# Two dense products per tile in the last full chunk, and a short last chunk that works on its five columns and rows alone

## The reference

```
x = layernorm(x + L0(x))     # three GCN convolutions with elu, then a linear map
W   = einsum('rb,bio->rio', w_comp, bases)              # 8 relations from 4 bases
msg = x[src] * edge_weight
agg = segment_sum(msg, edge_type * N + dst)             # per relation and node
x = layernorm(x + einsum('rni,rio->no', agg, W))
```

## Time and profile before

| | |
|---|---|
| time, median of 3 runs | 1186.85 us |
| profiled execution, its own time | 1187.31 us |
| its span (first to last instruction) | 1185.5 us |
| second layer's gathers, first start to last start | 541.0 to 1168.8 us |
| TensorE busy in 541 to 1170 us | 603.20 of 629.00 us |
| last output's norm on VectorE ends | 1182.72 us |

### The profile page before, as it was taken

The page is one execution under the profiler, slowest core; times in us unless marked ns, Lnnn a source line. Parts: engine busy times, 40 slices in busy tenths (PEclk is TensorE's granted clock), DMA queues, the critical chain, the costliest instruction groups (busy, mean ns, idle before and its releaser), DMA issues.

```text
span 1185.5 us, 21211 instructions
## 1 busy us (share of the span) xinstructions
PE 1076.2 (91%) x6601; PEld 833.6 (70%) x6604; DVE 836.3 (71%) x1992; ACT 684.9 (58%) x1716; POOL 543.1 (46%) x579
## 2 busy tenths in 40 slices
PE   2678888899999999977899999999999999999997
PEld 2565555566544644576788898888888888888885
DVE  4789889995566647787666767677676767767654
ACT  1598888984200310049666677677667767666740
POOL 5052000000132000005777777777777777777773
PEclk9778889999999999998999999999999999999999
DMA  6162000000200100214222212222222222222221
GB/s 165 34 233 92 1 2 1 1 1 1 66 23 12 49 7 4 60 35 112 53 53 58 58 52 58 57 56 53 57 56 55 55 57 55 53 58 55 57 54 36
DMA packets 49230, 60.66 MB, mean 51 GB/s; under 512 B 15255, under 2 KB 38841, under 8 KB 48502
## 3 DMA queue, kind: packets, MB, share of 16 engines
q0 software_dynamic: 17456, 36.02, 11.6%
q1 hardware_dynamic: 31686, 23.61, 6.8%
HBM read 46.30 MB, written 8.49 MB: 46 GB/s over the span
## 4 chain that ended last, share of the span: by engine, by line
PE 63%; DVE 12%; POOL 8%; issue 8%; DMA 3%; SPq 2%; ACT 2%; DVEq 1%; POOLq 0%; ACTq 0%
PE ps L1459 20%; PE ps L1605 13%; PE ps L1599 13%; PE ps L1585 11%; POOL arena L780 8%; DVE arena L1069 7%; PE ps L1448 2%; SPq L627 2%; DMA arena<-x_scratch,arena 1%; PE ps L1612 1%; PE ps L1618 1%; PE ps L1406 1%; DVE u L1268 1%; DMA dinv_col<-dinv_scratch 1%; DVE arena L1222 1%
## 5 line engine op out<-in xcount | busy, mean ns | idle before, releaser
L780 POOL DMA_INDIRECT arena<-x_scratch,arena x503 | 475.7, 946 | 191.2 <-issue 141.8
L1459 PE MATMUL ps<-arena,u 125*128 125x480 fp8e5 (+1 forms) x1575 | 361.7, 356 | 1.2 <-ACT arena L834 1.2
L1268 DVE SCALAR_TENSOR_TENSOR u<-ps,arena 128x200 f32<-128x200 f32 x600 | 213.6, 418 | 135.0 <-PE ps L1599 133.2
L1599 PE MATMUL ps<-u,dinv_all 128*125 128x200 f32 x1200 | 255.8, 336 | 25.2 <-ACT dinv_all L913 11.4
L1605 PE MATMUL ps<-arena 125*128 125x320 f32 x750 | 262.5, 432 | 0.0
L1599 PEld LDWEIGHTS ps<-u,dinv_all 128*125 128x125 f32 x1200 | 210.8, 189 | 63.8 <-issue 31.4
L1585 PE MATMUL ps<-hT,arena 128*128 128x192 f32 x1006 | 243.5, 331 | 11.9 <-DMA arena<-x_scratch,arena 11.4
L921 ACT COPY arena<-ps 125x400 f32<-125x400 f32 x300 | 144.1, 486 | 183.3 <-PE ps L1599 171.6
L1459 PEld LDWEIGHTS ps<-arena,u 125*128 125x128 bf16 x1575 | 153.2, 98 | 107.9 <-ACT arena L834 1.7
L1585 PEld LDWEIGHTS ps<-hT,arena 128*128 128x128 f32 x1006 | 179.0, 189 | 47.2 <-DMA arena<-x_scratch,arena 16.3
L1069 DVE TENSOR_TENSOR arena<-arena 128x2048 bf16<-128x2048 bf16 (+2 forms) x158 | 188.8, 1253 | 17.1 <-PE ps L1448 14.0
(11 more groups left out here) (174 smaller groups left out, 668.3 us busy)
## 6 DMA issues: line engine op xcount, KB each, us to landing
arena<-x_scratch,arena POOLq DMA_INDIRECT x503, 2.5
arena<-hT SPq DMA_DIRECT2D x3, 1562.5 KB, 7.1
edge_scratch<-arena SPq DMA_DIRECT2D x5, 403.0 KB, 4.9
arena<-in_x_dram SPq DMA_DIRECT2D x1, 1562.5 KB
dinv_all<-dinv_scratch SPq DMA_DIRECT2D x1, 1562.5 KB, 8.3
h_scratch<-hT SPq DMA_DIRECT2D x1, 1562.5 KB, 7.0
first_term_scratch<-arena SPq DMA_DIRECT2D x1, 1562.5 KB
arena<-first_term_scratch SPq DMA_DIRECT2D x1, 1562.5 KB
```

The costliest lines, as they stand in the source:

```text
L780: nc.gpsimd.indirect_dma_start(out=gat[:, j, :], out_offset=None, in_=x1_d, in_offset=bass.IndirectOffsetOnAxis(ap=idxg[:, j:j + 1], axis= ...
L1268: ins = V.scalar_tensor_tensor(movD[:, k % 2, i, :, :], ps[:, 4:5, 0:CODES].broadcast_to([P, NB, CODES]), hiD[:, ds(c * (4 * QD) + (4 * k ...
L1459: return T.matmul(ps[:, agg_bank(l, c), 0:CW[c]], u[0:BLK, s, k, :], region[:, s, 0:CW[c]], start=(first and s == 0 and k == 0), stop=(end ...
L1599: last = T.matmul(ps[0:BLK, 6 + w, at:at + NB * CODES], hotD[:, k % 2, i, :], movD[:, k % 2, i, :, :].rearrange("p b v -> p (b v)"), start ...
```

## The change

In chunk 14 two dense products stand behind each of the tiles 22 to 32, products 0 to 21; three are left for the last chunk, one behind each of its tiles 0 to 2. `finish_dense(14)` and `finish(14)` move from behind the last tile to behind tile 5. The last chunk's folding is done on its 5 columns (`few`), its four products have 5 stationary columns, and its statistics, root and norm are on 5 partitions; the folding is two additions behind each other into `few`, and `stats_dense(14)` and `norm_dense(14)` now stand ahead of it on VectorE. The looped chunks are the same.

The diff:

```diff
@@ scalar
                 copy_dense(DH - 1)
+                root_dense(DH - 1)
                 root(NCHK - 2)
-                root_dense(DH - 1)
-                root(NCHK - 1)
+                act.wait_ge(s_fv, NCHK)
+                nc.scalar.activation(fst[0:LNODES, 8:9], fst[0:LNODES, 7:8], ACT.Sqrt, bias=epst[0:LNODES, 0:1]).then_inc(s_fs, 1)
@@ vector
+                def stats_last():
+
+                    dve.wait_ge(s_fin, NCHK)
+                    yv = ystage[0:LNODES, 1, :]
+                    link(V.tensor_tensor(yv, ps[0:LNODES, 7, 0:D], x1r[0:LNODES, NCHK - 1, :], ALU.add))
+                    link(V.bn_stats(fst[0:LNODES, 0:6], yv))
+                    V.bn_aggr(fst[0:LNODES, 6:8], fst[0:LNODES, 0:6]).then_inc(s_fv, 1)
+
                 def norm_last():
...
                 ahead_of(C, 2)
+                stats_dense(DH - 1, 6)
                 stats(C - 1)
-                lower(C)
+                norm_dense(DH - 1, False)
+                few = aggf[:, :, 0:LNODES]
+                link(V.tensor_tensor(few, accN[0][:, :, AT:AT + LNODES], carry[:, :, 0:LNODES], ALU.add))
                 dve.wait_ge(s_mu, C * TB + -(-LTILES // BT))
-                V.tensor_tensor(aggf[:, :, 0:ABOVE], accN[2][:, :, 0:ABOVE], aggf[:, :, 0:ABOVE], ALU.add).then_inc(s_af, 1)
+                V.tensor_tensor(few, accN[2][:, :, 0:LNODES], few, ALU.add).then_inc(s_af, 1)
                 norm(C - 1, False)
-                stats_dense(DH - 1, 6)
-                norm_dense(DH - 1, False)
-                stats(C, 7)
+                stats_last()
                 norm_last()
@@ tensor
                         if rank >= 1 and j < DLEFT:
                             dense(TPB - DJ + j, 1 - half)
+                        if j == DJ:
+                            pe.wait_ge(s_se, c * (2 * QD) + 2 * QD)
                         if j >= DJ:
-                            if j == DJ:
-                                pe.wait_ge(s_se, c * (2 * QD) + 2 * QD)
-                            dense(j - DJ, half)
+                            for s in ((j - DJ,) if following else (2 * (j - DJ), 2 * (j - DJ) + 1)):
+                                dense(s, half)
...
                     tile(C, j, LTILES)
-                    for s in (2 * j, 2 * j + 1):
-                        if s < DLEFT:
-                            dense(TPB - DJ + s, 0)
-                    if j == LTILES - 1:
+                    if 2 * (TPB - DJ) + j < NBLK:
+                        dense(2 * (TPB - DJ) + j, 0)
+                    if j == 2 * BT - 1:
+                        finish_dense(DH - 1, 6)
                         pe.wait_ge(s_af, C)
                         pe.wait_ge(s_dv, DH - 1)
                         finish(C - 1)
-                finish_dense(DH - 1, 6)
                 pe.wait_ge(s_af, C + 1)
-                finish(C, 7)
+                for b in range(NB):
+                    last = T.matmul(ps[0:LNODES, 7, 0:D], aggf[:, b, 0:LNODES], basesS[:, b, :], start=(b == 0), stop=(b == NB - 1))
+                last.then_inc(s_fin, 1)
```

More of the change, by code:

```diff
@@ L1325, in norm @@
                     dve.wait_ge(s_y, c + 1)
+                def stats_last():
[4 more added lines that the diff above has]
+                    V.bn_aggr(fst[0:LNODES, 6:8], fst[0:LNODES, 0:6]).then_inc(s_fv, 1)
                 def norm_last():
                     dve.wait_ge(s_fs, NCHK)
-                    link(V.reciprocal(fst[:, 9:10], fst[:, 8:9]))
-                    V.tensor_scalar(gat[:, 0, :], ystage[:, 1, :], fst[:, 6:7], fst[:, 9:10], ALU.subtract, ALU.mult).then_inc(s_y, 1)
+                    link(V.reciprocal(fst[0:LNODES, 9:10], fst[0:LNODES, 8:9]))
+                    V.tensor_scalar(gat[0:LNODES, 0, :], ystage[0:LNODES, 1, :], fst[0:LNODES, 6:7], fst[0:LNODES, 9:10], ALU.subtract, ALU.mult).then_inc(s_y, 1)
                 def chunk(c, rank, following=TPB):
```

## The result

The changed kernel takes 1179.69 us (median of 22 runs, 1175.52 to 1184.39) against 1185.73 us of the kernel before (22 runs, 1180.13 to 1189.43). The ratio is 0.9953, with a 95% interval of 0.9940 to 0.9967: faster by 3.9 to 7.1 us. The profiled execution took 1179.80 us, with a span of 1178.0 us; before it was 1187.31 and 1185.5.

What follows compares the result with a forecast made beforehand. Gathers were taken to pace the second layer, TensorE to bound the last chunk's tiles, and VectorE the folding. Earlier folding (3.64) and the dense group's place (1.0) gave 4.63 us: 1186.85 - 4.6 = 1182.2 us, range 1181.3 to 1186.0.

Steps and rivals of the forecast that it cites:

- The bound: Second layer: gathers set the pace, one every 1.25 us, GpSimd never stopping; TensorE bounds from the last chunk's tile 0.
- The hidden products at tiles 22 and 23: Chunk 14: added products of two tiles end at 1153.35, hidden whole before tile 24 starts at 1153.82.
- the pairs at 1.41 us: From tile 24 on: a tile with two dense products takes 1.41 us; eight such tiles take 11.26.
- the clearing matmul at 0.22: Before the last chunk's tile 0: matmul clearing its bank over 512 columns takes 0.22 us, ends 0 and 0.54.
- the copy behind its cover: ScalarE's copy of the dense sum ends before `finish_dense(14)` wants it at 1171.28, with 0.3 us of cover.
- the additions at 0.18: Last chunk's folding on VectorE: two additions of 20 elements into `few`, 0.18 us each, bounds 0.16 and 0.60.
- the dense group's place on VectorE: End on VectorE: dense group's work no longer stands ahead of the last statistics, worth 1.0 of 4.63 us.
- The clock: Pause before the last products: clock holds; rival of half clock costs 1.2 us, within the eaten case's 0.12 chance.
- the slower rival: Tiles 24 to 32 and last chunk: open weight loads cost 21 products 8.0 us, time 1190.2; chance 0.03.
- That the backlog only moves: Rival: products fill no waits, last chunk's tile 0 starts 5.9 us later, time 1185.9; chance 0.06.
- half a us of the median's own scatter: Term of the forecast's own range, 1181.3 to 1183.2: half a us allowed for scatter of the measured median.
- 1186.85 as the point to subtract from: Median of the kernel before in us, from which the 4.6 us gain was taken to reach 1182.2.

Runs made afterwards that it cites:

- the move: Kernel before with only the dense products moved: 1178.61 us against 1182.61, ratio 0.9956; 13.2 us from the last gather's start to the end.
- the short chunk: Kernel before with only the last chunk's folding, products, statistics and norm cut to 5 columns or partitions: 1182.70 us, ratio 0.9994.
- the order of before: Changed kernel with both products with the bases behind the last tile and the dense group's statistics last on VectorE again: 1181.22 us, ratio 0.9973.
- the repeat: The changed kernel run and profiled again, unaltered, on the same chip as its parts: 1176.24 us, ratio 0.9947 to the kernel before.
- the fill: Kernel before plus 48 unused matmuls of ones at each of five places in the first layer: 1179.88 us against 1184.94, ratio 0.9962.

## Why the prediction came out as it did

**The bound** was right. The gathers run without a pause in all profiles but those of the slow chip, and no change behind them moved them: the gathers' step was 1.25 us in each.

**The hidden products at tiles 22 and 23, the pairs at 1.41 us, the clearing matmul at 0.22, the copy behind its cover, the additions at 0.18** all came out, each within 0.1 us. So did the sum, 4.63 us forecast and 4.7 measured from the last gather on, and its parts add up by themselves: 3.5 for the move, 0.8 to 0.9 for the short chunk, 0.4 for the order. The prediction divides its sum in another way, 3.64 for the earlier folding and 1.0 for the dense group's place on VectorE; with the order of before put back, only 0.4 was lost, so that second share overstates what the order is worth by itself. Two small sizes were off: tile 24's batch was 0.1 us later, and the last products took 1.04 us and not 1.16 (a weight load of five columns took 87 ns, one of 128 columns 192; I had kept that in the range only). One addition in the prediction is off by 0.04 us, without effect: 1170.49 and 0.43 make 1170.92 and not 1170.96.

**The clock** did not fall ahead of the last products: after 1.13 us of idling they take 1.04 us. The Trainium skill, "TensorE: Matmul & The Clock Gate", The HAM clock gate, has idleness bring the engine back to 1.2 GHz; here the clock behind the pause of 1.13 us was still 1.00 (in 1172 to 1174 us). The same section calls the number of slow matmuls at a kernel's start variable from run to run; in the first layer the traces agree in kind, with a wait of 2.97 us that was followed by the slow clock and one of 2.96 that was not.

**Weight loads** of pairs stay hidden (1.41 us a tile from 1159.15 on). The Trainium skill's sentence that a load overlaps a matmul only where row groups differ (same page, Part 3, The mechanism) does not hold for these full-row products: in 1155 to 1163 us of the changed kernel weight loads take 6.23 of the 8.00 us and matmuls all 8.00, and the slower rival that came from it falls. The same section also lets a load into a background weight buffer go ahead; whether these loads are of that kind no run shows. **That the backlog only moves** falls by the kernel with the move alone.

**The step that failed** is the last one: the term "half a us of the median's own scatter", and with it the choice of 1186.85 as the point to subtract from. Three runs of a kernel whose single runs spread over 9.3 us (1180.13 to 1189.43) don't fix a median to half a us. Over 22 runs the kernel before takes 1185.73, so 1.1 of the 2.5 us between 1182.2 and 1179.69 is that. The rest, 6.0 us between the medians against 4.6 forecast, lies inside the interval of the ratio (3.9 to 7.1 us): the medians do not tell 4.6 from 6.0. The measurement from the last gather on does, 4.7 in the profile pair and 4.8 in the repeat, and the estimate at an equal clock, 4.9 ± 0.9, points the same way. So the mechanism and its size were right, and the time fell below the range because the point of departure was 1.1 us too high and because 22 runs against 22 still leave 1.6 us either way. What spreads the runs is the clock in the first layer, shown by the fill: the same instructions plus idle matmuls, and the spread falls from 9.4 to 3.5 us. The term that measured 2.5 us had been put at 0.5, and the range should have reached lower by some 2 us; the profile had the sign of it in the windows of 150 to 250 us, with clocks of 0.93 and 0.90 beside the 1.00 of the stretch that I read. That idle time brings the falls is shown by the fill: in the four profiles that have it the clock shows no fall between 110 and 300 us; why the clock falls at such a wait in one execution and not in another stays open.

Of the profile pair's 2.8 us outside the change, 1.1 belong to the one profile of the kernel before, whose gathers took 947 ns in the median: the kernel with the filled first layer has the same second layer and takes 944 ns and 626.8 us for its 503. The other 1.7 lie ahead of the four waits, at all of which the clock fell in both profiles: the first matmul behind the first of them starts at 135.44 us before and already at 133.41 after, with mean clocks of 0.81 and 0.85 in 0 to 100 us. What made the one profile's gathers slower, and that clock differ, stays open.

## What to carry to other kernels

Measure a change at the end of a kernel from the last event that the change can't move (here the last gather's start): one profile then gave to 0.1 us what 44 runs gave to 1.6. Before stating a range, look at the granted clock of all stretches, not only of the one that is changed, since a far stretch with two possible clocks sets the spread of single runs. Six runs can also all fall on one side of it, so compare the clocks of the runs before their medians. And count the products that fill a wait, not the products that move: two in waits gave 0.9 us, three from one busy stretch to another nothing.

## What the runs showed of the hardware that was not expected

- A wait of 3 to 4 us on TensorE was followed by 1.2 GHz in some executions and not in others of the same code. 48 matmuls of ones (2.84 us) in each such wait kept the clock at 1.00 in 150 to 250 us, and the median was 5 us lower.
- Two outputs on SyncE's queue lie 0.95 us apart, though the second one's data had been ready for 2 us (the norm of line 1317 ends at 1171.80):

```profile
1172.88 0.35 SPq L701 DMA_DIRECT2D out_dram<-arena  x1
1173.83 0.88 SPq L703 DMA_DIRECT2D out_dram<-arena  x1
1175.14 0.28 SPq L705 DMA_DIRECT2D out_dram<-arena  x1
```

- Five partitions, 80 or 128 take VectorE nearly the same time for 128 elements: 0.28 us (L1332), 0.29 (L1307) and 0.29 (L1298).
- One chip ran the kernel before in 1337.7 us and not 1185. The two kernels profiled there had their first gather at 532.0 and 531.8 us, no later than elsewhere, and lost the time in the second layer.
